# Output projection kept in two PSUM banks over a batch element's 16 heads, and added to the residual once

## What is computed

```python
q = (layernorm(x) @ Wq).reshape(b, sq, H, HD) * (1.0 / np.sqrt(HD))
k = (ctx_2048 @ Wk).reshape(b, skv, H, HD)
v = (ctx_2048 @ Wv).reshape(b, skv, H, HD)
attn = softmax(einsum('bqhd,bkhd->bhqk', q, k), axis=-1)
c = einsum('bhqk,bkhd->bqhd', attn, v).reshape(b, sq, H * HD)
x = x + c @ Wo                       # the output projection and its residual
x = x + ffn(layernorm(x))            # silu(gate) * up, then down, block-quantised operands
```

## Time and profile before

| | |
|---|---|
| median of 3 runs | 2357.46 us (2356.16 to 2357.72) |
| span of the profiled execution, first to last instruction | 2354.9 us |
| PE busy in the span | 2232.6 us (95%) |
| DVE busy | 1852.0 us (79%) |
| ACT busy | 1100.8 us (47%) |
| POOL busy | 776.9 us (33%) |
| matmuls | 17486 |

### The profile page before, as it was taken

How to read it: one execution, slowest core, us unless ns; L and a number is a source line. 1 busy time by engine, 2 the same in 40 slices (tenths; PEclk the granted TensorE clock), 3 DMA queues, 4 the chain that set the end, 5 groups by cost and what they waited for, 6 DMA issues and landing times.

```text
span 2354.9 us, 58058 instructions
## 1 busy us (share of the span) xinstructions
PE 2232.6 (95%) x17486; PEld 1674.1 (71%) x17486; DVE 1852.0 (79%) x3711; ACT 1100.8 (47%) x2759; POOL 776.9 (33%) x1156
## 2 busy tenths in 40 slices
PE   7999999999999999999999999999999888888876
PEld 5778888888888888888888888888888533333333
DVE  7877777777777777777777777766666799999997
ACT  6744444444444444444444444444444445544543
POOL 4322222222222222222222222211100266666774
PEclk9999999999999999999999999999999999999999
DMA  5410101010101010101010101000000311111111
GB/s 199 146 37 24 44 22 40 22 40 22 42 22 40 22 40 22 40 22 42 22 41 24 44 23 40 18 28 10 28 5 14 129 50 53 49 53 53 49 53 45
DMA packets 49858, 101.37 MB, mean 43 GB/s; under 512 B 6112, under 2 KB 18912, under 8 KB 49824
## 3 DMA queue, kind: packets, MB, share of 16 engines
q1 hardware_dynamic: 39504, 68.70, 9.2%
q0 software_dynamic: 10320, 32.25, 4.4%
HBM read 77.86 MB, written 23.07 MB: 43 GB/s over the span
## 4 chain that ended last, share of the span: by engine, by line
PE 78%; DVE 14%; issue 6%; ACT 1%; DMA 0%; DVEq 0%; POOLq 0%; POOL 0%; SPq 0%; ACTq 0%
PE b_qk L997 28%; PE b_v L997 14%; PE b_o L997 14%; PE b_c L997 7%; PE b_s L997 7%; PE b_pt L1092 5%; DVE attn_weights L909 3%; DVE attn_weights L924 3%; DVE attn_weights L914 3%; DVE x_amax L838 1%; PE b_x L1004 1%; DVE prob L774 1%; DVE attn_weights L752 1%; DVE x_quantised L855 1%; PE b_o L1165 1%
## 5 line engine op out<-in xcount | busy, mean ns | idle before, releaser
L556 ACT ACTIVATE prob<-b_s,nmax 128x256 f32<-128x256 f32 x514 | 238.8, 469 | 536.3 <-DVE nmax L761 536.2
L997 PE MATMUL b_qk<-xT,attn_weights 128*128 (+1 forms) x3072 | 378.6, 273 | 0.0
L997 PE MATMUL b_qk<-kvT,attn_weights 128*128 (+1 forms) x3072 | 377.8, 273 | 0.0
L997 PE MATMUL b_v<-attn_weights,kvT 128*128 (+1 forms) x3072 | 377.3, 273 | 0.0
L997 PE MATMUL b_o<-attn_weights,cbuf 128*128 (+1 forms) x1536 | 373.5, 380 | 0.8 <-DVE acc L804 0.8
L997 PEld LDWEIGHTS b_qk<-xT,attn_weights 128*128 (+1 forms) x3072 | 300.6, 98 | 36.0
L997 PEld LDWEIGHTS b_qk<-kvT,attn_weights 128*128 (+1 forms) x3072 | 300.3, 98 | 35.7
L997 PEld LDWEIGHTS b_v<-attn_weights,kvT 128*128 (+1 forms) x3072 | 300.0, 98 | 35.3
L997 PEld LDWEIGHTS b_o<-attn_weights,cbuf 128*128 128x128 f16 x1536 | 149.9, 98 | 125.4 <-DVE acc L804 1.3
L365 POOL DMA_DIRECT2D kvrow<-kvt x61 | 34.7, 570 | 619.0 <-DVE kvT L686 619.0
L527 ACT ACTIVATE qk<-b_qk 128x512 f16<-128x512 f32 x256 | 152.8, 597 | 161.5 <-PE b_qk L997 161.5
(11 more groups left out here) (132 smaller groups left out, 3598.6 us busy)
## 6 DMA issues: line engine op xcount, KB each, us to landing
ffn_w<-wffn SPq DMA_DIRECT2D x48, 256.0 KB, 2.6
acc<-xtok POOLq DMA_DIRECT2D x16, 512.0 KB, 4.2
x_tiles<-x_scratch SPq DMA_DIRECT2D x32, 256.0 KB, 2.7
attn_weights<-x_scratch SPq DMA_DIRECT2D x32, 256.0 KB, 2.6
out<-attn_weights SPq DMA_DIRECT2D x32, 256.0 KB, 2.0
xrow<-xq POOLq DMA_DIRECT2D x61, 128.0 KB, 2.6
kvrow<-kvt POOLq DMA_DIRECT2D x61, 128.0 KB, 2.4
x_scratch<-acc POOLq DMA_DIRECT2D x15, 512.0 KB, 3.3
```

Of the source, the lines that this page charges most:

```text
L556: last = eng.activation(half(prob, q, 256), half(bS, q, 256), ACT.Exp, bias=nmax[:, q:q + 1], scale=1.0, accum_out=rsum[:, q:q + 1])
L997: last = eng.matmul(out, l, r, start=(a == 0), stop=(a == len(pairs) - 1))
```

## The change

The output projection now uses two banks, `o_bank = [bO, bW]`: even steps (first 128 tokens) accumulate in `b_o`, odd steps in `b_w`. In each bank the 48 matmuls of a batch element's eight products form one accumulation, started in quad 4s + 1 at step 0 or 1 and stopped in quad 4s + 4 at step 2 or 3. DVE adds each bank to `acc` once, at steps 2 and 3 of quad 4s + 4 (`ends=True`): 32 additions in place of 256. `pW` moves from `b_w` to the second half of bank `b_x`. The waits go with it: PE waits for `o_added` only at steps 0 and 1 of a batch element's first quad, POOL's and SP's stores count two additions per batch element, and the first feed-forward uses of `b_w` and `b_o` wait for the last additions.

So that start and stop flags are constants in the code, the loops are rewritten. PE: quads 0 to 8 and 53 to 64 are written out, and one loop over s = 2 to 12 has four quads (4s + 1 to 4s + 4) as its body: eleven passes, ten of which branch back. DVE: one loop over s = 1 to 11 with four quads in its body, the rest written out.

```diff
-        pW = bW[:, 0:256].bitcast(BF16)
+        pW = bX[:, 256:512].bitcast(BF16)
+        o_bank = [bO, bW]
...
-            eng.wait_ge(sm["o_added"], 4 * NQ + 4)
+            eng.wait_ge(sm["o_added"], 2 * B)
...
-                            wait_apart(eng, "o_added", 16 * s + 4)
+                            wait_apart(eng, "o_added", 2 * s)
...
-                    if isinstance(n, int) and n == 0:
-                        eng.sem_inc(sm["o_added"], 1)
-                    else:
+                    if ends and k >= 2:
+
+                        s = n // QPB - 1
                         eng.wait_ge(sm["o_done"], i + 1)
-                        eng.wait_ge(sm["o_added"], i)
-                        if k == 0:
-                            eng.wait_ge(sm["acc_loaded"], 16 * (((n - 1) >> 2) + 1))
-                        a = acc[:, bass.ds((((n + 3) >> 2) & 1) * (2 * D) + (k % 2) * D, D)]
-                        eng.scalar_tensor_tensor(out=a, in0=bO[:, :], scalar=O_OUT, in1=a, op0=ALU.mult, op1=ALU.add
-                                                 ).then_inc(sm["o_added"], 1)
+                        if k == 2:
+                            eng.wait_ge(sm["acc_loaded"], 16 * (s + 1))
+                        a = acc[:, bass.ds(((s + 1) & 1) * (2 * D) + (k % 2) * D, D)]
+                        eng.scalar_tensor_tensor(out=a, in0=o_bank[k % 2][:, :], scalar=O_OUT, in1=a, op0=ALU.mult,
+                                                 op1=ALU.add).then_inc(sm["o_added"], 1)
...
-            quad(FFN_FROM, ffn=True)
-            with eng.Fori(FFN_FROM + 1, FFN_TO) as n:
-                quad(n, ffn=True)
-            with eng.Fori(FFN_TO, NQ - 4) as n:
-                quad(n)
+            quad(FFN_FROM, ffn=True, ends=True)
+            with eng.Fori(1, FFN_TILES // QPB) as s:
+                for q in range(1, QPB + 1):
+                    quad(QPB * s + q, ffn=True, ends=(q == QPB))
+            for n in range(FFN_TILES + 1, NQ - 2):
+                quad(n, ffn=(n < FFN_TO), prepare=(n < NQ - 4), ends=(n % QPB == 0))
...
-                    eng.wait_ge(sm["o_added"], i)
+                    if place == 1 and k < 2 and (not isinstance(batch, int) or batch > 0):
+                        eng.wait_ge(sm["o_added"], 2 * batch - 1 + k)
...
-                    last = product(bO[:, :], [
+                    pairs = [
...
+                    for at, (l, r) in enumerate(pairs):
+                        last = eng.matmul(o_bank[k % 2][:, :], l, r, start=(place == 1 and k < 2 and at == 0),
+                                          stop=(place == 0 and k >= 2 and at == len(pairs) - 1))
...
-            with eng.Fori(1, QPB) as n:
+            for n in range(1, QPB):
                 ready(n)
                 quad(n, fresh=True)
...
-            with eng.Fori(FFN_FROM + 2, FFN_TO + 1) as n:
-                ready(n)
-                quad(n, ffn=True)
-            with eng.Fori(FFN_TO + 1, NQ - 4) as n:
-                ready(n)
-                quad(n)
-            with eng.Fori(NQ - 4, NQ) as n:
-                quad(n, prepare=False)
+            for q in range(1, QPB + 1):
+                ready(FFN_FROM + q)
+                quad(FFN_FROM + q, ffn=True)
+            with eng.Fori(2, FFN_TO // QPB) as s:
+                for q in range(1, QPB + 1):
+                    ready(QPB * s + q)
+                    quad_at(QPB * s + q, s, q % QPB, ffn=True)
+            for n in range(FFN_TO + 1, NQ):
+                if n < NQ - 4:
+                    ready(n)
+                quad(n, prepare=(n < NQ - 4))
```

More of the change, by code:

```diff
@@ L753, in inner, with quad @@
                                   ).then_inc(sm["inner_done"], 1)
-            def quad(n, front=True, split=0, ffn=False, prepare=True):
+            def quad(n, front=True, split=0, ffn=False, prepare=True, ends=False):
                 w = n - FFN_FROM
@@ L880, in _ @@
             quad(QPB - 1, split=QUAD // 2)
-            quad(FFN_FROM, ffn=True)
-            with eng.Fori(FFN_FROM + 1, FFN_TO) as n:
-                quad(n, ffn=True)
-            with eng.Fori(FFN_TO, NQ - 4) as n:
-                quad(n)
-            quad(NQ - 4, prepare=False)
-            quad(NQ - 3, prepare=False)
+            quad(FFN_FROM, ffn=True, ends=True)
[4 more added lines that the diff above has]
+                quad(n, ffn=(n < FFN_TO), prepare=(n < NQ - 4), ends=(n % QPB == 0))
             quad(NQ - 2, prepare=False)
@@ L892, in _ @@
             quad(NQ - 1, prepare=False)
-            quad(NQ, front=False, prepare=False)
+            quad(NQ, front=False, prepare=False, ends=True)
             def pair_tile(t):
@@ L1032, in quad, with quad_at @@
             def quad(n, front=True, fresh=False, ffn=False, prepare=True):
+                q = n % QPB if isinstance(n, int) else None
+                quad_at(n, (n + QPB - 1) // QPB - 1, q, front, fresh, ffn, prepare)
+            def quad_at(n, batch, place, front=True, fresh=False, ffn=False, prepare=True):
                 xb, kb = par_tile(xT, n), par_tile(kvT, n)
@@ L1103, in quad @@
                         eng.wait_ge(sm["c_lo"], min(i, 4 * NQ + 2))
-                    last = product(bO[:, :], [
+                    pairs = [
                         (cbuf[:, (s * 2 + a) * 256 + (k % 2) * P:(s * 2 + a) * 256 + (k % 2 + 1) * P],
                          attn_w(n, b, O_AT[s // 2] * PIECE + (s % 2) * 512, 512))
-                        for s in (2 * (k // 2), 2 * (k // 2) + 1) for a, b in PARTS])
+                        for s in (2 * (k // 2), 2 * (k // 2) + 1) for a, b in PARTS]
+                    for at, (l, r) in enumerate(pairs):
+                        last = eng.matmul(o_bank[k % 2][:, :], l, r, start=(place == 1 and k < 2 and at == 0),
+                                          stop=(place == 0 and k >= 2 and at == len(pairs) - 1))
                     last.then_inc(sm["o_done"], 1)
@@ L1134, in _ @@
             quad(FFN_FROM)
-            ready(FFN_FROM + 1)
-            quad(FFN_FROM + 1, ffn=True)
-            with eng.Fori(FFN_FROM + 2, FFN_TO + 1) as n:
-                ready(n)
-                quad(n, ffn=True)
-            with eng.Fori(FFN_TO + 1, NQ - 4) as n:
-                ready(n)
-                quad(n)
-            with eng.Fori(NQ - 4, NQ) as n:
-                quad(n, prepare=False)
+            for q in range(1, QPB + 1):
[9 more added lines that the diff above has]
+                quad(n, prepare=(n < NQ - 4))
             quad(NQ, front=False, prepare=False)
@@ L1153, in inner_transpose @@
                     eng.wait_ge(sm["i_moved"], c0 - 1)
+                elif c0 == 1:
+                    eng.wait_ge(sm["o_added"], 2 * B)
                 for c in range(4):
@@ L1163, in down @@
                     eng.wait_ge(sm["d_moved"], t)
+                elif k == 0:
+                    eng.wait_ge(sm["o_added"], 2 * B - 1)
                 for c in range(4):
```

## The result

The changed kernel takes 2369.28 us (2368.53 to 2370.43) beside 2357.1 us for the kernel before in the same comparison: a ratio of 1.0053, 95% interval 1.0039 to 1.0067. It is 12.2 us slower. The time lies within the range given, but on the side of rival B, not of the forecast 2354.9.

The account below looks back on a forecast made before the run. PE's matmuls were taken to bound steady attention and DVE the feed-forward stage; gains of 1.7 us at the start and 0.8 at the end, everything else 0, took 2357.46 to 2354.9 us, range 2352.2 to 2376.

Parts of the forecast that it names:

- rival B: PE's branch back, ten times: the four-quad body doesn't fit and must be fetched; 2359 to 2375 us, 0.36 above its deciding point.
- The additions: DVE in steady attention: 224 additions removed, 153.7 us of DVE time, about 210 of them worth 0.
- The start: Step 1 of quads 1, 2 and 3: PE's waits for prob shrink by 0.7, 0.7 and 0.3 us, sum 1.7.
- The end: Quad 64, step 2: PE's product no longer waits 0.79 us for the addition before it; gain 0.8 us.
- Two banks, `pW`, new waits: PE's projection matmuls, pW in b_x and the waits for o_added and acc_loaded: each costed at 0.
- Longer code: PE's loop body of 2127 instructions: price 0 if it stays on the chip, the choice for the sum; otherwise rival B.
- deciding point: Rival B at PE's branch back: counts as slower from 0.7 us shown per branch, a fetch of 2.9 us; chance above it 0.36.
- the sequencer's lead: At PE's loop branch the sequencer runs 2.4 us ahead, which was said to cover most of a fetch.
- 0.4 to 2.0: Rival B's loss in us shown on PE per missed branch, from fetches of 2.6 to 4.2 us.
- 4 to 20: Rival B's total loss in us on PE over ten branches back.
- its sign: Rival B in steady attention: nine or ten PE instruction packets per pass, and a PE gap every 114.6 us behind L1146.

Follow-up runs that it names:

- e8: Kernel before, with the two banks in quad 64 alone (steps 1 and 3 go to b_w): 2356.11 us beside 2356.75, ratio 0.9998.
- e2: Changed kernel with PE's attention written out without a loop, 31896 instructions on PE: 2355.48 us, ratio 0.9990.
- e3: Changed kernel with two banks but accumulation over two quads, 64 additions, and a PE loop body of two quads (1222 instructions): 2353.76 us, ratio 0.9985.
- e7: Changed kernel with 190 semaphore increments in front of PE's first work, moving the long loop's place in the instruction packets: 2436.95 us, ratio 1.0344.
- e4: Changed kernel with PE's loop over eight quads per body (3984 instructions, four branches back): 2360.47 us, ratio 1.0017.
- e5: Kernel before, with PE's long loop given a body of three quads (1830 instructions, fourteen branches back): 2445.99 us, ratio 1.0378.
- e1: Kernel before, one bank and all 256 additions, with only PE's loop made a four-quad body (2126 instructions): 2385.09 us beside 2356.74, ratio 1.0114.

## Why the prediction was wrong

**The additions.** Right. DVE lost 129 us of busy time and nothing came of it in steady attention: other than the gaps of the loop, the pace is 28.65 us per quad in every version with all its matmuls (quad 45 alone takes up to 0.4 more in some).

**The start.** Right: 1.7 us was the sum, and quads 1 to 3 became 1.57 us shorter. In the changed kernel ACT idles 0.26 us before the exponential of quad 1 in place of 0.82, and PE waits 1.06 us in place of 1.61, in quads 2 and 3 1.03 and 0.80 in place of 1.58 and 1.12:

```profile
53.01 1.23 DVE L687 SCALAR_TENSOR_TENSOR attn_weights<-stage,attn_weights 128x1024 f32 x1 [0.51 <-ACT attn_weights L536]
...
54.16 0.68 DVE L762 TENSOR_REDUCE nmax<-b_s 128x2 f32<-128x512 f32 x1
...
54.87 0.47 ACT L557 ACTIVATE prob<-b_s,nmax 128x256 f32<-128x256 f32 x1 [0.26 <-DVE nmax L762]
...
59.13 0.66 PE L1096 MATMUL b_pt<-ident,prob 128*128 128x128 f32 x4 [1.06 <-DVE prob L775]
```

Step 1 of quad 1 gains 0.55 and not 0.7, because DVE now comes to its weight piece before ACT has written the high part, and waits 0.51 us for it (first line); POOL has no part in that, since the two `prob` of this step last 2.95 us as before (2.94). The rest of quad 1's 0.69 us lies in step 0.

**The end.** The wait of 0.79 us is gone, and the last addition comes 0.96 us earlier (e8), where 0.8 had been given. Right up to there; behind it the runs scatter by more than that.

**Two banks, `pW`, new waits.** Right at 0: the projection's matmuls take 379 ns in place of 380, and e2 and e3 run dense.

**Longer code.** Here the prediction failed, at the sentence "If it does, the price is 0, which is my choice for the sum." It does not stay. I had the count (2127 instructions), the figure of the Trainium skill's page (2048) and its rule that gave the mechanism, and still gave the case above its deciding point 0.36, because I trusted the sequencer's lead to cover the fetch. By the rows then at hand that rule of the Trainium skill deserved the larger chance: nothing in the trace spoke for a store of more than the 612 instructions seen to be held.

The size of rival B was worked out well, but one term was missing. It asked for a fetch of more than 2.9 us and took the kernel's own DMAs, 2.6 to 4.2 us, as the bounds. The branch takes 3.3 to 3.9 us. It starts 2.5 us before the next scores are due, as the prediction had it, but its end is not yet work: in quad 12 it ends at 388.99 + 3.29 = 392.28 us, and the scores start 0.55 us later, at 392.83. So PE loses 1.35 to 1.95 us each time, in place of 0.9 to 1.5 without that term; "0.4 to 2.0" had been given. Ten of them make 15.9, the upper half of "4 to 20". The ten packets per pass are what B had named as its sign. What B did not contain, and the changed kernel escaped by luck, is the second packet: had the loop begun elsewhere, it would have lost some 59 us (15.7 + 43.7, by e7). DVE's body of four quads, which B counted in, is innocent: it stands in e2 and e4 as well, where PE runs dense but for its own branches, and no branch on DVE lasts over 0.5 us.

The Trainium skill's page "Runtime: NRT & Kernel Launch", section "Instruction fetch mechanics", says that a taken branch whose target isn't in the current window of two pages must fetch its target before it goes on. The runs agree on the fetch, with branches of 3.3 to 4.4 us for it, and not on the two pages: the body of 1506 instructions, over seven packets, branches back in 0.21 us. The same section gives 2048 instructions for PE. No run contradicts that size (seven packets are held, nine are not), but as a bound for the length of a body it is too high: the 1830 instructions of e5 are not held, as they touch nine packets.

## What to carry to other kernels

Before a loop is made longer to get constants into its body, count the body's instructions on that engine, each matmul twice, and the packets that they touch, and keep it under what a run has shown to be held; on PE here 1506 in seven packets was fine and 1830 in nine was not. If the body must be longer, write it out or take fewer and longer passes, since the price is per taken branch, and look for a second gap just behind it, which the loop's place in the program decides. And work taken from an engine that bounds nothing is worth only what the few places show where another engine waits for it: here 2.5 us (1.57 in the start, 0.96 at the end) for 129 us of DVE's busy time.

## What the runs showed of the hardware that was not expected

A loop's cost can hang on its place in the program: 190 instructions put in front moved it by 4.4 us per pass. The packet behind the branch's target is not fetched along with it; it starts 0.66 to 1.26 us after the branch's end, and a second gap of 0.9 to 2.8 us follows if the target stands near its packet's end (8, 17 and 38 instructions before it in e7, e5 and e1; none at 198). In e5 TensorE's granted clock fell to 0.50 for 6.8 us after 2.1 us of idling and 0.6 of work. A semaphore increment on PE's sequencer cost about 0.12 us (22 us for 190) and did not hide in front of the first wait.
